# Attention heads packed two by two into 64-row tiles of the matrix array

## The chip, the cores and the metric

The kernel runs on one core of a Trainium2 chip. The metric is the device time of one execution in microseconds (us), the median of three runs. TensorE multiplies matrices, VectorE and ScalarE read its results from PSUM (eight banks of 128 partitions x 512 fp32), GpSimd works between SBUF tiles, and the sync engine issues almost all transfers.

## The reference

Two cross-attention layers follow each other on the same eight batches (B = 8, 256 query rows, C = 320, 20 heads of 16, a context of 256 rows of 512). The first 77 context rows (layer 0) or the first 252 (layer 1) are text, the rest are image rows with weights of their own.

```python
# layer 0
out_text = attend(q, k, v); out_ip = attend(q, k_ip, v_ip)      # softmax(q k^T / 4) v, 20 heads
x = (out_text + out_ip) @ Wo.T + bo + x
# layer 1
probs_t = softmax(q @ k_t.T / 4)
qsem = l2norm(probs_t @ text)                                    # 512 wide, per head and row
fused = q @ k_ip.T / 4 + 0.5 * (qsem @ l2norm(ip).T)
probs_ip = softmax(fused) * spatial_mask
x = (probs_t @ v_t + probs_ip @ v_ip) @ W_out + b_out + x
```

## The kernel before

A unit u is one batch in one layer: units 0 to 7 are layer 0 (L = 0), units 8 to 15 layer 1. Each unit is cut into ten slots j, one for a pair of heads; q = 10 u + j counts the pairs. plan(u, j) writes out by hand what every engine does in a slot, and each engine walks through the same plan and takes its own part: scores of pair q + 1, maxima of unit u + 1, `weigh` (probabilities times values, every second slot, four heads in four 32-column tiles), `weights` (exponentials), in layer 1 `quad` (the quadratic form behind the norm of qsem), 'bg' pieces of the projections of unit u + 2 (PACE says how many matmuls), `back` (transposes of the values' result), and the parts of unit u - 1 that end it ('ot', 'op' and others). 'shift' is the transposition of the maxima of unit u + 1.

Precision: a projected query or key is kept as a rounded part and the rest (hi and lo). The three products hi x hi, hi x lo and lo x hi stand one below the other as 3 x 16 = 48 rows per head. Head a of a pair has rows 48 a to 48 a + 47 of KP (keys) and of QP (queries); QP holds the two heads in two column blocks with zeros in the other head's rows, so that one matmul with 96 rows multiplies one head. Rows 96 to 99 hold the row maxima (mhi, mlo) in QP and indicators in KP: with them a matmul with 100 rows gives scores less the maximum. QP's zeros are set by GpSimd once (L1209, L1218), and rows 96 to 99 are filled with a large value at the start of layer 1 (L1241).

Lines that the change and the prediction's steps touch: L427 maxima (two matmuls of 256 columns per head), L438 transposes of the maxima, L450 scores (two matmuls of 512 columns per pair, one for each half of the keys, both heads side by side), L464 quad, L482, L486, L491 and L496 weigh, L505 back, L348 projections, L546 and L548 output. ScalarE's exponentials are L768 (rounded, PH, layer 1) and L778 (P). VectorE reduces maxima in L971 and L972 (layer 0) or L974 and L976 (layer 1) and multiplies Y by the quads in L989. GpSimd subtracts PH from P in L1198 and raises norms to the power -0.5 in L1205. On the sync queue L1294 sends the maxima into QP, L676 and L684 load packed queries and keys of unit u + 2 from DRAM, where L654 and L656 have stored them. A unit's loads come in three chunks m: pairs 0 to 3, 4 to 7, 8 and 9.

PSUM: one bank belongs to weigh, seven form a pool. take() gives the free bank that was given back longest ago and waits until its last reader is done; give() is called when the last matmul is issued. The bank of a projection is held from its first matmul to the next job's, so six take turns for the rest. A bank of scores is free when P is written, one of maxima after VectorE's second operation, one of a quad after L989, one of transposes after normalization, one of a Q projection after VectorE's lower part.

```python
MAXH = (3, 3, 3, 3, 3, 3, 2, 0, 0, 0)      # heads of maxima in each slot
MAXF = (2, 2, 2, 2, 2, 2, 2, 2, 2, 2)      # the same before unit 0
SHIFT = 7                                  # slot in which the maxima are transposed
...
bank = min((b for b in pool if id(b) not in held), key=lambda b: at.get(id(b), 0))
```

## Time and profile before

| | us |
|---|---|
| median of three runs | 886.08 (885.2 to 886.97) |
| the profiled execution | 881.61 |
| its span, first to last instruction | 879.8 |
| TensorE busy | 809.0 |
| VectorE busy | 556.6 |
| ScalarE busy | 428.3 |
| GpSimd busy | 340.7 |

The mean granted TensorE clock is 0.963 of full speed. Busy shares overlap between engines. The ends of matmuls are modelled and reach into the next ones, so the distance from one start to the next tells more than a duration.

### The profile page before, as it was taken

The numbers are of one execution on the slowest core, as the hardware profiler recorded it, in microseconds if no ns is written. First come the engines' busy times: TensorE is split into PE (matmuls) and PEld (weight loads), VectorE is DVE, ScalarE is ACT, GpSimd is POOL, SyncE is SP. The second block draws the span as 40 slices with busy tenths as digits, with TensorE's granted clock in tenths as the row PEclk, the third lists the DMA queues.
The fourth block names the chain that finished last, engine by engine and source line by source line (L and its number), as shares of the span: only waits on it lengthen the run. The fifth ranks groups of instructions, "written<-read, shape, count | busy, mean of one in ns | idle before, by whom it ended". The sixth has DMA issues, their size and how long they took to land.

```text
span 879.8 us, 17377 instructions
## 1 busy us (share of the span) xinstructions
PE 809.0 (92%) x6456; PEld 653.0 (74%) x6456; DVE 556.6 (63%) x1569; ACT 428.3 (49%) x922; POOL 340.7 (39%) x255
## 2 busy tenths in 40 slices
PE   5759799898989898999999999999999999989896
PEld 5758597676867677778787877877878778767575
DVE  4447254555555657576867848669678586596654
ACT  5234433535353536545545655455465554545451
POOL 6311101101010103031657547365384473665763
PEclk9889889999999999999999999999999999999799
DMA  9953922737262737374516234143053321401010
GB/s 267 245 125 103 213 85 64 189 116 184 70 173 81 186 97 190 95 197 113 140 39 162 85 85 122 58 110 121 26 139 97 86 83 58 111 1 34 1 30 16
DMA packets 102116, 96.71 MB, mean 110 GB/s; under 512 B 10152, under 2 KB 102032, under 8 KB 102032
## 3 DMA queue, kind: packets, MB, share of 16 engines
q1 hardware_dynamic: 100976, 94.61, 40.2%
q8 instruction: 52, 0.85, 0.4%
q10 hardware_dynamic: 1056, 0.98, 0.4%
q14 instruction: 32, 0.26, 0.1%
HBM read 57.71 MB, written 36.70 MB: 107 GB/s over the span
## 4 chain that ended last, share of the span: by engine, by line
PE 67%; DVE 9%; SPq 7%; DMA 5%; issue 5%; ACT 4%; POOL 2%; ACTq 0%; POOLq 0%; DVEq 0%
PE pB L348 19%; PE pB L464 10%; PE pB L427 7%; PE pB L450 6%; PE pB L546 5%; DMA KP<-k0d 4%; PE pPV L486 4%; PE pPV L491 3%; PE pPV L496 3%; DVE m_sb L974 3%; SPq L1294 3%; PE pPV L482 2%; PE pB L505 2%; ACT P L778 2%; POOL Y L1198 2%
## 5 line engine op out<-in xcount | busy, mean ns | idle before, releaser
L1198 POOL TENSOR_TENSOR Y<-P,wv 128x512 f32<-128x512 f32 x120 | 153.6, 1296 | 206.0 <-ACT P L778 205.9
L989 DVE TENSOR_TENSOR Y<-pB,Y 128x512 f32<-128x512 f32 x160 | 109.0, 686 | 96.0 <-PE pB L464 71.0
L427 PE MATMUL pB<-KP,QP 96*128 96x256 f32 x640 | 133.8, 292 | 25.4 <-DMA KP<-k0d 24.5
L427 PEld LDWEIGHTS pB<-KP,QP 96*128 96x128 f32 x640 | 109.1, 194 | 40.2 <-issue 18.9
L450 PE MATMUL pB<-QP,KP 100*128 100x512 f32 x320 | 114.7, 436 | 17.0 <-DMA QP<-mlo 14.2
L974 DVE TENSOR_REDUCE m_sb<-pB 128x2 f32<-128x504 f32 x160 | 108.0, 676 | 14.2 <-PE pB L427 12.4
L778 ACT ACTIVATE P<-pB 128x512 f32<-128x512 f32 x160 | 86.2, 594 | 45.9 <-PE pB L450 45.9
L1175 POOL TENSOR_TENSOR klo<-xin,khi 128x256 fp32r<-128x256 f32 x18 | 13.1, 751 | 245.5 <-ACT khi L691 245.5
L691 ACT ACTIVATE Vs<-pPV 128x512 f32<-128x512 f32 (+1 forms) x80 | 39.4, 492 | 139.0 <-PE pPV L486 106.5
L971 DVE TENSOR_REDUCE m_sb<-pB 128x2 f32<-128x154 f32 x160 | 50.0, 313 | 86.9 <-PE pB L427 86.0
L778 ACT ACTIVATE P<-pB,ln 128x512 f32<-128x512 f32 x160 | 101.3, 693 | 0.0
L768 ACT ACTIVATE wv<-pB 128x512 fp32r<-128x512 f32 x120 | 66.6, 590 | 56.0 <-PE pB L450 53.4
L972 DVE TENSOR_REDUCE m_sb<-pB 128x2 f32<-128x358 f32 x160 | 83.3, 520 | 0.0
L464 PE MATMUL pB<-wv,wk 128*128 128x512 f32 x250 | 78.3, 417 | 0.4
L348 PE MATMUL pB<-chi,wki 128*128 128x180 f32 (+3 forms) x384 | 72.0, 276 | 0.0
L450 PEld LDWEIGHTS pB<-QP,KP 100*128 100x128 f32 x320 | 52.9, 196 | 24.7 <-DMA QP<-mlo 16.1
L348 PE MATMUL pB<-khi,wq 128*128 128x256 f32 (+1 forms) x288 | 59.0, 307 | 8.5 <-DVE wq L893 8.5
L348 PE MATMUL pB<-wvi,chi 128*128 128x320 f32 x256 | 62.1, 314 | 0.4 <-POOL wvi L1188 0.4
L1205 POOL TENSOR_TENSOR rn<-n,mhalf 128x8 f32<-128x8 f32 (+2 forms) x17 | 57.4, 3379 | 11.7 <-DVE n L1020 11.7
L348 PEld LDWEIGHTS pB<-chi,wki 128*128 128x128 f32 (+1 forms) x384 | 56.8, 174 | 6.5 <-issue 4.5
L464 PEld LDWEIGHTS pB<-wv,wk 128*128 128x128 f32 x250 | 45.0, 194 | 19.5 <-issue 10.7
L348 PEld LDWEIGHTS pB<-khi,wq 128*128 128x128 f32 (+1 forms) x288 | 46.6, 195 | 14.0 <-DVE wq L893 8.5
(174 smaller groups left out, 1693.7 us busy)
## 6 DMA issues: line engine op xcount, KB each, us to landing
QP<-q0d SPq DMA_DIRECT2D x64, 192.0 KB, 4.1
KP<-k0d SPq DMA_DIRECT2D x64, 192.0 KB, 4.5
c_sb<-in_cT SPq DMA_DIRECT2D x16, 512.0 KB, 4.8
q0d<-qhi SPq DMA_DIRECT2D x32, 256.0 KB, 2.5
k0d<-khi SPq DMA_DIRECT2D x30, 256.0 KB, 2.5
q0d<-qlo SPq DMA_DIRECT2D x16, 256.0 KB, 2.8
k0d<-klo SPq DMA_DIRECT2D x15, 256.0 KB, 2.7
QP<-q1d SPq DMA_DIRECT2D x32, 96.0 KB, 4.3
```

What stands on the lines that cost most here:

```text
L348: made = mm(out, l, r, start=(n == 0), stop=(n == len(pairs) - 1))
L427: made = mm(bank[:, sc * S:sc * S + S], QP[i][0:KROWS, j, a, sc * 128:sc * 128 + 128], KP[i][0:KROWS, j, :], start=True, stop=True)
L450: mm(bank[:, :], KP[i][0:QROWS, j, ch * 128:ch * 128 + 128], QP[i][0:QROWS, j, :, :].rearrange("p a s -> p (a s)"), start=True, stop=True) ...
L464: made = mm(bank[:, :], G[i][:, col:col + 128], ph[src], start=(n == 0), stop=(n == len(jobs) - 1))
L768: act(PH[q % HR][ch], bank_of["sc", q, ch][:, :], ACT.Exp, scale=0.25).then_inc(ac_ph, 1)
L778: act(P[:, q % PR, ch, :], bank_of["sc", q, ch][:, :], ACT.Exp, scale=0.25, **twice).then_inc(ac_exp, 1)
L971: nc.vector.tensor_reduce(m_sb[:, :, h], v[:, :, 0:TXT0], AX, ALU.max)
L972: nc.vector.tensor_reduce(m_sb[:, :, H + h], v[:, :, TXT0:S], AX, ALU.max).then_inc(dv_mx, 1)
L974: nc.vector.tensor_reduce(m_sb[:, :, h], v[:, :, 0:TXT1], AX, ALU.max)
L989: tt(Y[:, p, dst, :], bank_of["gp", q, dst][:, :], Y[:, p, dst, :], MUL).then_inc(dv_y, 1)
L1198: tt(Y[:, p, ch, :], P[:, p, ch, :], PH[q % HR][ch].bitcast(F32), SUB).then_inc(po_y, 1)
L1205: tt(rn[:, :, hs], n2[:, :, hs], mhalf[:, 0:2 * n].rearrange("p (c h) -> p c h", c=2), POW).then_inc(po_rn, 1)
```

## The change

Each head of a pair gets half of the array's rows: head 0 rows 0 to 63, head 1 rows 64 to 127. KROWS becomes 48 and QROWS 52 per head, QP loses its zeros and its second column block, and every matmul of scores and maxima names a tile of 64 rows (tile_position). Each head has a PSUM bank of its own, which holds both halves of its keys (scores) or of its queries (maxima). So scores are four matmuls of 256 columns instead of two of 512, maxima four of 256 for a pair as before. Both banks of a pair are taken before its first matmul.

The order in a slot becomes scores, maxima, weigh, quads, projections, with the maxima of two heads together (MAXH and MAXF count pairs), two pairs in slots 0 and 1, one in slots 2 to 7. SHIFT goes from 7 to 8. The loads of chunks 0 and 1 stand in slot 8 of the sync program, chunk 2 stays in slot 9. Exponentials and GpSimd's difference work on one head of both key halves instead of both heads of one half, so VectorE's product waits for both differences. PH gets a tile of its own. The maxima of both heads of a pair go into QP with one DMA per row kind, two partitions each. GpSimd's three kinds of memset of QP go; an indicator of -1e20 and a row of ones take the place of the large value. Weight columns are ordered so that the four pairs of a chunk lie side by side in DRAM.

```diff
--- before.py
+++ after.py
@@ -20,8 +20,8 @@
 EC = 4
 NG = 5
 NP = H // 2
-KROWS = 96
-QROWS = 100
+KROWS = 48
+QROWS = 52
 PR = 3
 HR = 2
...
-MAXH = (3, 3, 3, 3, 3, 3, 2, 0, 0, 0)
-MAXF = (2, 2, 2, 2, 2, 2, 2, 2, 2, 2)
-SHIFT = 7
+MAXH = (2, 2, 1, 1, 1, 1, 1, 1, 0, 0)
+MAXF = (1,) * 10
+SHIFT = 8
...
-    heads = [("max", u + 1, h) for h in range(sum(many[:j]), sum(many[:j + 1]))] if u + 1 < U else []
-    first, rest = heads[:1], heads[1:]
+    pairs = [("max", u + 1, p) for p in range(sum(many[:j]), sum(many[:j + 1]))] if u + 1 < U else []
     out = []
     if 0 <= u < U - 1 and j == SHIFT:
         out += [("shift", u + 1)]
     scores = [("scores", q + 1)] if u >= 0 and q + 1 < U * NP else []
     weigh = [("weigh", *divmod(q // 2 - 1, NG))] if q >= 2 and q % 2 == 0 else []
     weigh += [("weights", q + 1)] if scores else []
+    out += scores + pairs + weigh
     if u >= B:
-        out += scores + weigh + [("quad", q, 0)] + first + [("quad", q, 1)]
-    else:
-        out += scores + first + weigh
-    out += pieces[0] + pieces[1] + rest[:1] + pieces[2] + rest[1:]
+        out += [("quad", q, 0), ("quad", q, 1)]
+    out += pieces[0] + pieces[1] + pieces[2]
     if q >= 2 and q % 2 == 0:
         out += [("back", *divmod(q // 2 - 1, NG))]
...
-        QP = [sb(f"QP{i}", [128, NP, 2, S], F32R) for i in range(2)]
+        QP = [sb(f"QP{i}", [128, NP, S], F32R) for i in range(2)]
         KP = [sb(f"KP{i}", [128, NP, S], F32R) for i in range(2)]
...
-        PH = [[flat(wv)[:, 896 + 512 * i:896 + 512 * i + 512] for i in range(2)], [flat(w)[:, at:at + 512] for w, at in ((wv, 1920), (wk, 1792))]]
+        PH = sb("PH", [128, HR, 2, 2 * S], F32R)
...
         def ind_ready(u):
             u = u if u < 2 else B + u % 2 if u >= B else u % 2
-            return l_ind[u], 16
+            return l_ind[u], 64 if u >= B else 32
...
-            def maximum(u, h):
-                i, j, a = u % 2, h // 2, h % 2
-                bank = take("mx", u * H + h)
-                pe.wait_ge(*pack_landed(u, h // 8))
-                pe.wait_ge(po_set, 2 + u % 2)
+            def maxima(u, j):
+                i = u % 2
+                banks = [take("mx", u * H + 2 * j + a) for a in range(2)]
+                pe.wait_ge(*pack_landed(u, j // 4))
                 for sc in range(2):
-                    made = mm(bank[:, sc * S:sc * S + S], QP[i][0:KROWS, j, a, sc * 128:sc * 128 + 128],
-                              KP[i][0:KROWS, j, :], start=True, stop=True)
-                made.then_inc(pe_mx, 1)
-                give(bank)
+                    for a in range(2):
+                        rows = slice(64 * a, 64 * a + KROWS)
+                        made = mm(banks[a][:, sc * S:sc * S + S], QP[i][rows, j, sc * 128:sc * 128 + 128],
+                                  KP[i][rows, j, :], start=True, stop=True, tile_position=(64 * a, 0))
+                        if sc == 1:
+                            made.then_inc(pe_mx, 1)
+                            give(banks[a])
...
+                banks = [take("sc", q, a) for a in range(2)]
                 for ch in range(2):
-                    bank = take("sc", q, ch)
-                    mm(bank[:, :], KP[i][0:QROWS, j, ch * 128:ch * 128 + 128],
-                       QP[i][0:QROWS, j, :, :].rearrange("p a s -> p (a s)"), start=True, stop=True).then_inc(pe_sc, 1)
-                    give(bank)
+                    for a in range(2):
+                        rows = slice(64 * a, 64 * a + QROWS)
+                        made = mm(banks[a][:, ch * S:ch * S + S], KP[i][rows, j, ch * 128:ch * 128 + 128],
+                                  QP[i][rows, j, :], start=True, stop=True, tile_position=(64 * a, 0))
+                        if ch == 1:
+                            made.then_inc(pe_sc, 1)
+                            give(banks[a])
...
-                ph = PH[q % HR]
...
-                    made = mm(bank[:, :], G[i][:, col:col + 128], ph[src], start=(n == 0), stop=(n == len(jobs) - 1))
+                    made = mm(bank[:, :], G[i][:, col:col + 128], PH[:, q % HR, src, :], start=(n == 0), stop=(n == len(jobs) - 1))
...
         def head_rows(dram, m):
             chunk = dram[m // 2][m % 2]
-            return chunk.rearrange("z (d j a) s -> (z d) j a s", a=2, d=D)
...
         def load_queries(engine, dma, u, m):
             i, js = u % 2, slice(4 * m, min(4 * m + 4, NP))
             engine.wait_ge(l_q, 96 * (u + 1))
-            engine.wait_ge(po_set, 2 + i)
             if u >= 2:
                 engine.wait_ge(pe_sc, 2 * ((u - 2) * NP + js.stop))
             for a in range(2):
-                dma(QP[i][48 * a:48 * a + 48, js, a, :].bitcast(F32), head_rows(qd[u], m)[:, :, a, :]).then_inc(l_ld[i][m], 16)
+                dma(QP[i][64 * a:64 * a + KROWS, js, :].bitcast(F32), head_rows(qd[u], m)[:, a]).then_inc(l_ld[i][m], 16)
...
-                dma(KP[i][48 * a:48 * a + 48, js, :].bitcast(F32), head_rows(kd[u], m)[:, :, a, :]).then_inc(l_ld[i][m], 16)
...
             def rounded_weights(q):
                 k = q - B * NP
-                for ch in range(2):
-                    ac.wait_ge(pe_sc, 2 * q + ch + 1)
+                for a in range(2):
+                    ac.wait_ge(pe_sc, 2 * q + a + 1)
                     ac.wait_ge(pe_gp, 2 * (k - HR) + 2)
                     ac.wait_ge(po_y, 2 * (k - HR) + 2)
-                    ac.wait_ge(pe_bg, job_no(B - 1, "V2"))
-                    act(PH[q % HR][ch], bank_of["sc", q, ch][:, :], ACT.Exp, scale=0.25).then_inc(ac_ph, 1)
+                    act(PH[:, q % HR, :, S * a:S * a + S], two(bank_of["sc", q, a], 128, 2), ACT.Exp, scale=0.25).then_inc(ac_ph, 1)
...
                 twice = {"bias": ln2[:, 0:1]} if q >= B * NP else {}
-                for ch in range(2):
-                    ac.wait_ge(pe_sc, 2 * q + ch + 1)
+                for a in range(2):
+                    ac.wait_ge(pe_sc, 2 * q + a + 1)
                     ac.wait_ge(pe_pv, (q - PR) // 2 + 1)
                     ac.wait_ge(lo_w["ki0"], 1)
                     ac.wait_ge(lo_w["v0"], 1)
                     ac.wait_ge(dv_set, 1)
-                    act(P[:, q % PR, ch, :], bank_of["sc", q, ch][:, :], ACT.Exp, scale=0.25, **twice).then_inc(ac_exp, 1)
+                    act(P[:, q % PR, :, S * a:S * a + S], two(bank_of["sc", q, a], 128, 2), ACT.Exp, scale=0.25,
+                        **twice).then_inc(ac_exp, 1)
...
             def maximum(u, h):
-                n = u * H + h
+                n, col = u * H + h, h % 2 * NP + h // 2
                 v = bank_of["mx", n][:, :].rearrange("p (c t) -> p c t", c=2)
                 dv.wait_ge(pe_mx, n + 1)
                 dv.wait_ge(pe_sr, u)
                 if u < B:
-                    nc.vector.tensor_reduce(m_sb[:, :, h], v[:, :, 0:TXT0], AX, ALU.max)
-                    nc.vector.tensor_reduce(m_sb[:, :, H + h], v[:, :, TXT0:S], AX, ALU.max).then_inc(dv_mx, 1)
+                    nc.vector.tensor_reduce(m_sb[:, :, col], v[:, :, 0:TXT0], AX, ALU.max)
...
             def quad(q, dst):
                 k, p = q - B * NP, q % PR
                 dv.wait_ge(pe_gp, 2 * k + dst + 1)
-                dv.wait_ge(po_y, 2 * k + dst + 1)
+                dv.wait_ge(po_y, 2 * k + 2)
                 tt(Y[:, p, dst, :], bank_of["gp", q, dst][:, :], Y[:, p, dst, :], MUL).then_inc(dv_y, 1)
...
                         if what == "max":
-                            maximum(*a)
+                            for h in range(2):
+                                maximum(a[0], 2 * a[1] + h)
...
             def weights(q):
                 k, p = q - B * NP, q % PR
-                for ch in range(2):
-                    po.wait_ge(ac_exp, 2 * q + ch + 1)
-                    po.wait_ge(ac_ph, 2 * k + ch + 1)
+                for a in range(2):
+                    ss = slice(S * a, S * a + S)
+                    po.wait_ge(ac_exp, 2 * q + a + 1)
+                    po.wait_ge(ac_ph, 2 * k + a + 1)
                     po.wait_ge(pe_pv, (q - PR) // 2 + 1)
                     po.wait_ge(lo_w["k1"], 1)
                     po.wait_ge(lo_w["v1"], 2)
-                    tt(Y[:, p, ch, :], P[:, p, ch, :], PH[q % HR][ch].bitcast(F32), SUB).then_inc(po_y, 1)
+                    tt(Y[:, p, :, ss], P[:, p, :, ss], PH[:, q % HR, :, ss].bitcast(F32), SUB).then_inc(po_y, 1)
...
-            nc.gpsimd.memset(QP[0][:, :, :, :].bitcast(F32), 0.0).then_inc(po_set, 1)
-            po.wait_ge(po_set, 2)
...
-            po.wait_ge(lo_w["vi0"], 1)
-            nc.gpsimd.memset(QP[1][:, :, :, :].bitcast(F32), 0.0).then_inc(po_set, 1)
-            po.wait_ge(po_set, 3)
...
-                    if u in (B - 1, B) and j == 3:
-                        po.wait_ge(pe_sc, 2 * u * NP)
-                        po.wait_ge(*((lo_c, 4 * (B + 2)) if u < B else (po_y, 10)))
-                        nc.gpsimd.memset(QP[(u + 1) % 2][KROWS:QROWS, :, :, :].bitcast(F32), 1e20).then_inc(po_big, 1)
-                        po.wait_ge(po_big, u - B + 2)
...
-                sp.wait_ge(po_set, 2 + i)
...
-                dma(KP[i][KROWS:QROWS, :, :].bitcast(F32),
-                    ind[:, L, None, :].to_broadcast([4, NP, S]).bitcast(F32)).then_inc(l_ind[u], 16)
+                for a in range(2):
+                    dma(KP[i][64 * a + KROWS:64 * a + QROWS, :, :].bitcast(F32),
+                        ind[:, L, None, :].to_broadcast([4, NP, S]).bitcast(F32)).then_inc(l_ind[u], 16)
+                    if L:
+                        sp.wait_ge(dv_set, 1)
+                        dma(QP[i][64 * a + KROWS + 2:64 * a + KROWS + 3, :, :].bitcast(F32),
+                            ones[0:2 * NP, :]).then_inc(l_ind[u], 16)
...
-                sp.wait_ge(po_set, 2 + i)
-                if u in (B, B + 1):
-                    sp.wait_ge(po_big, u - B + 1)
-                rows = [(96, mhi, 0), (98, mhi, H), (97, mlo, 0), (99, mlo, H)] if u < B else [(96, mhi, 0), (97, mlo, 0)]
+                rows = [(0, mhi, 0), (2, mhi, H), (1, mlo, 0), (3, mlo, H)] if u < B else [(0, mhi, 0), (1, mlo, 0)]
                 for r, tile, h0 in rows:
                     sp.wait_ge(ac_sr, u + 1)
                     if tile is mlo:
                         sp.wait_ge(dv_sr, u + 1)
-                    dma(QP[i][r:r + 1, :, :, :].bitcast(F32), tile[h0:h0 + H, :].bitcast(F32)).then_inc(l_m[i], 16)
+                    dma(QP[i][KROWS + r:128:64, :, :].bitcast(F32), tile[h0:h0 + H, :].bitcast(F32)).then_inc(l_m[i], 16)
...
-                    if u + 2 < U and j == NP - 1:
-                        for m in range(KC):
+                    for m in ((0, 1) if j == 8 else (2,) if j == NP - 1 else ()):
+                        if u + 2 < U:
                             load_queries(sp, dma, u + 2, m)
                             load_keys(sp, dma, u + 2, m)
-                        if u + 2 in (1, B, B + 1):
-                            load_ind(u + 2)
+                    if u + 2 in (1, B, B + 1) and j == NP - 1:
+                        load_ind(u + 2)
...
-    ind[2, 1, TXT1:S] = -1.0
+    ind[2, 1, TXT1:S] = -1e20
...
-    order = _np.concatenate([_np.arange(128 * m, min(128 * m + 128, C)).reshape(-1, D).T.reshape(-1) for m in range(3)])
+    order = _np.concatenate([_np.arange(128 * m, min(128 * m + 128, C)).reshape(-1, 2, D).transpose(2, 1, 0).reshape(-1)
+                             for m in range(3)])
     P = lambda a: _np.ascontiguousarray(a[:, order])
```

## Rows read from the trace of the kernel before

**Rows 1.** The page, part 1: busy time, share of the span, instructions.

```profile
PE 809.0 (92%) x6456; PEld 653.0 (74%) x6456; DVE 556.6 (63%) x1569; ACT 428.3 (49%) x922; POOL 340.7 (39%) x255
```

**Rows 2.** Windows: length, busy PE, PEld, DVE, ACT, POOL, clock, DMA share, GB/s.

```profile
247.00:291.00 44.00, 39.55 (x343) 32.56 (x343) 24.89 (x74) 20.17 (x45) 4.83 (x8) 0.96 0.47 127
...
643.00:701.00 58.00, 57.83 (x453) 46.09 (x451) 41.58 (x118) 31.05 (x67) 31.85 (x22) 1.00 0.33 93
```

**Rows 3.** The waits: who for whom, us in total, times, longest.

```profile
PE pB L427 <- DMA KP<-k0d: 24.5, 8, 5.3
...
PE pB L450 <- DMA QP<-mlo: 14.2, 8, 5.4
```

**Rows 4.** The chain in order of time: start, us, engine and line, matmuls.

```profile
430.82 0.24 PE pB L427 x2
...
432.22 0.47 PE pB L450 x2
...
508.47 0.43 PE pB L548 x2
...
510.37 0.86 PE pPV L496 x16
```

**Rows 5.** Timeline of PE at start-up: start, us, line, form, count.

```profile
16.79 0.38 PE L348 MATMUL pB<-chi,wki 128*128 128x180 f32 x2
...
17.13 0.38 PE L348 MATMUL pB<-chi,wki 128*128 128x180 f32 x2
```

**Rows 6.** Timeline of PE in slot 6 of unit 9, from full array to column tiles and back.

```profile
508.98 0.39 PE L450 MATMUL pB<-QP,KP 100*128 100x512 f32 x1
509.30 1.07 PE L491 MATMUL pPV<-P,VY 128*32 128x256 f32 x16
510.18 1.05 PE L496 MATMUL pPV<-Y,y 128*32 128x256 f32 x16
511.16 1.21 PE L464 MATMUL pB<-wv,wk 128*128 128x512 f32 x4
```

**Rows 7.** Timeline, all engines, end of unit 4 and start of unit 5.

```profile
279.66 0.38 PE L438 MATMUL pB<-ident,m_sb 128*40 128x128 f32 x2 [0.90 <-DVE m_sb L972]
...
281.95 0.62 PE L450 MATMUL pB<-QP,KP 100*128 100x512 f32 x2
...
283.42 1.47 SPq L1294 DMA_DIRECT2D QP<-mlo  x2
...
286.29 2.08 SPq L684 DMA_DIRECT2D KP<-k0d  x2
...
286.64 0.73 PE L450 MATMUL pB<-QP,KP 100*128 100x512 f32 x2 [0.54 <-DMA QP<-mlo]
...
288.08 0.62 PE L450 MATMUL pB<-QP,KP 100*128 100x512 f32 x2
...
291.72 0.47 PE L427 MATMUL pB<-KP,QP 96*128 96x256 f32 x2 [3.02 <-DMA KP<-k0d]
```

**Rows 8.** The page, part 6: DMA issues, KB each, median us to landing.

```profile
KP<-k0d SPq DMA_DIRECT2D x64, 192.0 KB, 4.5
...
k0d<-khi SPq DMA_DIRECT2D x30, 256.0 KB, 2.5
```

**Rows 9.** Timeline of DVE, two heads of maxima in layer 0.

```profile
263.86 0.32 DVE L971 TENSOR_REDUCE m_sb<-pB 128x2 f32<-128x154 f32 x1
...
264.53 0.31 DVE L971 TENSOR_REDUCE m_sb<-pB 128x2 f32<-128x154 f32 x1
```

**Rows 10.** Timeline, all engines, slots 9 and 0 around unit 12.

```profile
644.61 5.54 POOL L1205 TENSOR_TENSOR rn<-n,mhalf 128x32 f32<-128x32 f32 x1 [0.58 <-DVE n L1020]
...
650.13 3.79 POOL L1198 TENSOR_TENSOR Y<-P,wv 128x512 f32<-128x512 f32 x3
...
651.52 0.69 DVE L989 TENSOR_TENSOR Y<-pB,Y 128x512 f32<-128x512 f32 x1 [2.41 <-POOL Y L1198]
...
652.52 0.91 PE L450 MATMUL pB<-QP,KP 100*128 100x512 f32 x2
```

9 lines of the change are left out of this document (6 added, 3 removed).

## The prediction

> **What bounds the kernel now.** I read the busy shares of the page first, then the windows by unit, then the chain of waits, then single slots of the timeline. TensorE is busy 92% of the span, no other engine above 63% [rows 1]. By windows the two halves differ: a layer-0 unit of 44.0 us has TensorE busy 39.55 us, a layer-1 unit 57.83 of 58.00 us, with VectorE at 41.58 and GpSimd at 31.85 [rows 2]. So in layer 1 every matmul taken away is time, until another wait appears; in layer 0 there are about 4.5 us of waits per unit that two DMA chains and a reduction set: eight waits each for packed keys (24.5 us) and for shift rows (14.2 us) [rows 3]. TensorE is thus the engine to shorten, and the question is what comes late once it is shorter.
>
> **Matmuls removed.** The chain shows two score matmuls (512 columns) in 0.47 us and the two of one head's maxima (256 columns) in 0.24 us: 0.235 and 0.12 us each [rows 4]. After the change both kinds are four matmuls of 256 columns per pair of heads, in two row tiles. If the two tiles run at once, each four cost 2 x 0.12 = 0.24 us. Scores: 160 pairs x (0.47 - 0.24) = 37 us. Maxima: 160 pairs x (0.48 - 0.24) = 38 us. Together -75 us.
> Row tiles are nowhere in this trace, so the cost is bounded. Low end: column tiles, 16 fp32 matmuls of 256 columns in 0.86 us [rows 4], that is 0.054 us each; one such matmul alone takes 0.215 us (L548: two in 0.43 us), so four stream at once. Upper end: weight loads that don't overlap. Matmuls of 180 columns with a full load of 128 columns each come every 0.11 us (three from 16.79 to 17.13 [rows 5]), though by their columns (0.12 us for 256) they would need 0.085: the load paces them. Four such loads in a row would be 0.45 us. I take 0.24 us, since the column rows are of the same kind and show loads and matmuls of different tiles starting together.
> The Trainium skill ("TensorE: Matmul & The Clock Gate", Part 3, The mechanism) states that a weight load overlaps matmuls in flight only where its row group differs, and that matmuls of different row tiles start about 4 ns apart. By it the four would take 0.24 us and the sum stays at -75; by loads in a row as in [rows 5] it would be -8. No row here shows a row tile.
>
> **Mode changes added.** From the last score matmul (508.98) to the first column-tiled one (509.30) are 0.32 us instead of 0.235; the way back, L496 at 510.18 to L464 at 511.16, is 0.98 us for four quads of 0.22: about 0.09 us each way [rows 6]. Now a unit changes to column tiles and back five times, 10 changes. Afterwards each of the ten slots enters row tiles, five go on to column tiles and then to full, five go straight to full: 25. Fifteen more x 16 units + 20 in unit -1 = 260 x 0.09 = +23 us. TensorE's work: -52 us, about 3.35 us per unit.
>
> **Layer 0: shift and loads.** Rows around 280 us, between units 4 and 5 [rows 7]. The transposes of the maxima (L438) start at T = 279.66, the shift DMAs come behind the key stores of the slot before (the mlo pair at 283.42), and scores(u+1, 0) starts at 286.64 = T + 7.0 after a wait of 0.54. The loads stand directly behind the shift rows in sync's order, so already now they are issued right after them: the loop moves them to slot 8, but SHIFT moves to slot 8 too, so nothing is sooner; all is one slot later on TensorE's count. After the change T is the start of slot 8: the key stores are out of the way, mhi is ready about T + 0.8 (an estimate: transpose 0.38 and a copy of 40x256, 0.4), four DMAs of 0.75 us each (1.47 for two) are issued by T + 4.0, the last from T + 3.25, and it lands 2.45 us later as now (half into the x2 row, 284.2, to 286.64): T + 5.7, perhaps 0.4 more, since each of them now writes two partitions instead of one, which no row shows. TensorE's slot 8 lasts 4.1 us (281.95 to 286.64 less 0.54), so it waits 1.6 to 2.0 instead of 0.54: +1.2. Keys: Q, Q, K, K at 0.65 us each (1.25 for two are 0.62 and a pause) from T + 4.0; the second K is issued at T + 6.0 and lands 4 us later (4.5 is the median [rows 8]; in the row here 287.8 to 291.7), T + 10.0. TensorE is there at T + 5.7 + 1.44 (slot 9, 286.64 to 288.08) + 0.24, T + 7.4: a gap of 2.6 for 3.02. Rows of four heads are now contiguous in DRAM, so packets may grow; stores of 256 KB land in 2.5 us against 4.5 for these 192 KB [rows 8], so between 0 and 2 us could come off; I take none, since the loads queue behind each other either way. L438's own wait, 0.90, should fall to 0.3, as the last pair is now ahead of eleven background matmuls.
> Slots 0 and 1 now hold four heads each (MAXH 2, 2). VectorE takes 0.67 us a head (263.86 to 264.53 [rows 9]). By the rule of take(), the oldest free bank of seven with one held by the background chain, the fourth maximum of slot 1 gets the bank of the transposes that closed slot 0 (free after their normalization, for which I take 0.9 us, between one head's maxima and two [rows 9]; wait 0.4), and the pair of slot 2 gets a bank of Qa, whose low part VectorE writes behind the four maxima: 0.9 + 4 x 0.67 + 0.68 = 4.3 us into a slot that TensorE leaves after about 3.4: 0.9 us. Sum per unit: +1.2 - 0.4 - 0.6 + 0.4 + 0.9 = +1.5, for the seven steady units, with some 2 us for the first ones: +12 us.
>
> **Layer 1: the same two slots.** In slot 0 of unit 12, which ends at 652.52, GpSimd's power takes 5.54 us, so that the differences Y of one pair (1.26 us each) are ready only at 651.4 and 652.7, and VectorE's product waits 2.41 us for the first [rows 10]. After the change the halves are heads, each product needs both, and the first comes 1.3 us later. TensorE in slot 0: weigh starts after the maxima, ScalarE's P comes behind weigh's evacuation, and the second quad needs the bank of the first score: about 0.5 us. In slot 1 the first pair waits for the banks of both products, the second for the transposes that are normalized behind them: with the slot's start at 652.9, the products done at 653.4 and 654.1 and the bank free at 654.85 (0.75 later, the same estimate without its sum), TensorE loses 0.25 us before the first pair and 1.1 before the second. The old order loses about 0.45 us in that slot as well, where its first quad needs the bank of the last product. The keys of the next unit: issued by T + 4.5, landing T + 8.5, wanted at T + 8.1: 0.4. Per unit 0.5 + 1.35 - 0.45 + 0.4 = +1.8, six units: +11 us. VectorE does not become the bound over a whole unit: 41.6 us of work in some 56 [rows 2]. Units 14 and 15, which wait for GpSimd now: the later product costs 0.7 us in some five places, +3 us.
> The memsets of QP on GpSimd go; in the start-up ScalarE and the loads set the time and nothing waits for them, so 0. ScalarE's and GpSimd's operations on two pieces of 256 instead of one of 512 keep their elements; I take 0 (ScalarE's share, 49% [rows 1], would cover some per cent).
>
> **Sum.** -75 + 23 + 12 + 11 + 3 = -26 us. The profiled execution has 879.8 us of span and 881.61 in all; the median of the runs is 886.08. -26 of 881.6 is 855.6; the runs lie 4.5 higher: 860, and since the waits were counted in the busiest places only, 862.
>
> **Rivals.** (a) The tiles don't overlap, or their weight loads don't. For: a 128-column load alone is 0.11 us and each half tile loads 128 columns. Against: the column tiles. Then scores and maxima gain 0.02 to 0.03 us a pair, 8 us at most, and changes and waits stay: -8 + 23 + 26 = +41, 927 us.
> (b) The slower side with the mechanism intact: the rotation of banks. Scores and two pairs take six of seven banks at once in slots 0 and 1, so TensorE runs at the pace of VectorE's reductions (0.67 us a head) and of ScalarE's exponentials. I have 1.5 to 1.8 us per unit; from 3.35 us per unit the change gives nothing. If the lag reaches slot 2 and weigh waits for the products too, 4 us per unit x 15 = 60 against 52: +8, 894 us. For: two fronts of four maxima, 2.7 us of VectorE ahead of the products. Against: VectorE idles there now (2.41 us ahead of the product [rows 10]).
> The Trainium skill ("TensorEngine Tiling (Array Packing)", Gotcha 1) states that row tiling raises the pressure on PSUM because row tiles write different banks; that speaks for this rival, and no row of the kernel before shows how much.
> (c) The waits are mostly covered: larger packets end the key gap 1 us sooner and VectorE fills its idle time with maxima. Waits of +8 instead of +26: -44, 842 us.
> (d) That the loads come a slot sooner, as the change says: then layer 0 would lose its key gap, 3 us x 7, and end at 862 - 18 = 844, which is (c)'s time by another way; sync's order speaks against it, so its chance is counted in (c)'s.
>
> **How the numbers follow.** The forecast -26 has a chance of 0.58, with its own range of 848 to 876; (c) 0.15, (b) 0.12, (a) 0.15. Runs of this kernel differ by about 0.2%, 1.8 us, which is what can be told from no change. Of the forecast's case 0.03 ends within that; so faster 0.70, same 0.03, slower 0.27. The range reaches from (c) to (b) and leaves (a) out: 840 to 896.
>
> **What would show it.** L427 and L450 (as they are renumbered) in the chain: four matmuls in 0.24 us means tiles at once; 0.45 means loads in a row. The gap before the first key-dependent maximum in layer 0 near 2.6 us, the gap before scores(u+1, 0) near 1.8. In layer 1 TensorE's share falls from 0.997 to about 0.97 in a unit of 57, with the loss in slot 1. If that slot is no longer than before, (c) holds; if VectorE's products end the waits of weigh, (b).

## The result and the profile after

The changed kernel takes 892.4 us (median of 8 runs, 887.9 to 893.7) beside 886.4 us (8 runs of the kernel before in the same session, 882.9 to 889.2): a ratio of 1.0066, 95% interval 1.0045 to 1.0087. It is slower; the forecast was 862 us, 3% faster. The profiled executions stand a little further apart than the medians: 892.19 us with a span of 890.4 against 881.61 with 879.8, +10.6 us. The accounts below are of these two. Of one kernel below, grouped, two of the four executions were over 1.5% above its fastest: its median (1015.3 us) is of all four, its ratio of the other two.

Lines are renumbered by the change: scores are L452, maxima L426, transposes of the maxima L438, quads L467, projections L346.

The page of the changed kernel, busy time and share, answers to [rows 1]:

```profile
PE 791.7 (89%) x6776; PEld 607.8 (68%) x6776; DVE 554.5 (62%) x1569; ACT 433.1 (49%) x922; POOL 321.8 (36%) x251
```

TensorE is busy 17 us less, where 52 were forecast, and its share falls by three points, so waits have come in. The windows of one whole unit each (from the first score matmul of a unit to that of the next; length, busy PE, PEld, DVE, ACT, POOL, granted clock, DMA share, GB/s) answer to [rows 2]. First the kernel before, unit 5 and unit 13:

```profile
286.64:330.60 43.96, 39.54 (x343) 32.71 (x343) 26.04 (x77) 20.88 (x47) 4.19 (x6) 0.96 0.51 141
701.87:760.63 58.76, 58.59 (x460) 46.85 (x459) 42.28 (x120) 31.34 (x68) 32.60 (x23) 1.00 0.29 79
```

and the same units of the changed kernel:

```profile
283.33:326.82 43.49, 39.06 (x365) 30.36 (x365) 25.90 (x78) 21.19 (x47) 4.14 (x7) 0.92 0.56 143
709.68:768.95 59.27, 57.15 (x478) 44.18 (x477) 42.35 (x119) 31.52 (x67) 32.44 (x23) 1.00 0.32 80
```

In layer 1 TensorE works 1.44 us less per unit, not 3.35, and idles 1.95 us more. In layer 0 it gains 0.5 us, and its mean clock falls from 0.96 to 0.92. TensorE's waits (engine, tile and line, releaser: total us, times, longest) answer to [rows 3]:

```profile
PE pB L426 <- DMA KP<-k0d: 25.0, 10, 5.7
PE pB L452 <- DMA QP<-mlo: 21.8, 9, 8.5
...
PE pB L426 <- DVE qlo L895: 4.0, 7, 0.6
PE pB L426 <- DVE Y L991: 3.5, 6, 2.0
...
PE pB L467 <- DVE alo L895: 3.0, 5, 1.2
PE pB L426 <- DVE ST L1016: 3.0, 5, 0.7
PE pB L426 <- DVE klo L895: 2.8, 5, 0.6
PE pB L438 <- DVE m_sb L974: 2.7, 7, 0.6
...
PE pB L467 <- ACT P L779: 2.5, 6, 0.7
PE pB L426 <- DVE tb L1009: 2.3, 8, 0.3
```

The wait for shift rows grew by 7.6 us against [rows 3], and seven kinds of wait behind VectorE and ScalarE that hardly existed before make 21.1 us (4.0 + 3.5 + 3.0 + 3.0 + 2.8 + 2.5 + 2.3); the wait ahead of the transposes (L438) fell from 6.1 to 2.7. All idle times of TensorE over 0.25 us together are 94.1 us, before 66.0: +28.

**What a mode change costs.** Slot 9 of unit 7 has no maxima and the same six background matmuls in both kernels. Timeline of PE (start, us, line, form, count), before:

```profile
411.05 0.71 PE L450 MATMUL pB<-QP,KP 100*128 100x512 f32 x2
411.60 0.28 PE L348 MATMUL pB<-chi 128*128 128x256 f32 x1
...
412.32 0.63 PE L450 MATMUL pB<-QP,KP 100*128 100x512 f32 x2
```

and after:

```profile
412.59 0.50 PE L452 MATMUL pB<-QP,KP 52*128 52x256 f32 x4 [0.17 <-DMA QP<-mlo]
413.03 0.39 PE L346 MATMUL pB<-chi 128*128 128x256 f32 x1
413.25 0.28 PE L346 MATMUL pB<-clo,chi 128*128 128x256 f32 x1
413.37 0.28 PE L346 MATMUL pB<-chi,clo 128*128 128x256 f32 x1
...
413.73 0.28 PE L346 MATMUL pB<-chi,clo 128*128 128x256 f32 x1
413.94 0.50 PE L452 MATMUL pB<-QP,KP 52*128 52x256 f32 x4
```

Background matmuls of 256 columns follow each other every 0.12 us (413.25 to 413.37). The first one after the row tiles is followed by the second only after 0.22 us (413.03 to 413.25), and the first tile matmul starts 0.21 us after the last full one (413.73 to 413.94). A change thus costs twice: about 0.1 us ahead of the first matmul in the new mode, and 0.1 us again ahead of the second. The slot is 1.35 us for 1.27: the scores take 0.235 us less and two changes come, 0.16 us each here, because the kernel before has a pause of its own in this slot, behind the transposes (411.05 to 411.60 is 0.55 us for two matmuls of 0.235). In the other slots read this way it is up to 0.20 us. The medians of all such steps at full clock in the changed kernel's trace agree: 0.21 us for 0.12 up to the first matmul in the new mode, 0.22 for 0.12 up to the second (from column tiles back to quads 0.34 for 0.23). Counted in the traces, PE changes its mode 160 times before and 419 times after: 259 more.

**The half clock.** Windows of one microsecond of the changed kernel in slot 0 of unit 4, after TensorE idled from 242.9 to 245.2 for packed keys (columns as above; the granted clock is the third last):

```profile
245.00:246.00 1.00, 0.80 (x12) 0.70 (x16) 0.29 (x2) 0.00 (x0) 1.00 (x2) 0.91 1.09 217
246.00:247.00 1.00, 1.00 (x12) 0.45 (x13) 1.00 (x4) 0.00 (x0) 0.11 (x1) 0.50 1.03 209
...
249.00:250.00 1.00, 1.00 (x9) 1.00 (x9) 0.00 (x0) 1.00 (x3) 0.00 (x0) 0.89 1.08 284
250.00:251.00 1.00, 1.00 (x10) 0.88 (x8) 0.00 (x0) 0.29 (x1) 0.00 (x0) 1.00 0.23 69
```

Some 3.4 us run at 0.50, the lower of the clock's two levels (1.2 GHz instead of 2.4), once the wait is over; the price is about half of that. Other stretches of the changed kernel behind waits for keys last 6.8 us. The kernel before has 3.4 us behind four of its six waits for keys in units 2 to 7, and none behind those of units 6 and 7 (2.80 and 2.56 us). Over the span the granted clock is 0.963 before and 0.950 after: (1 - 0.963) x 879.8 = 32.6 us of full-speed time lost against (1 - 0.950) x 890.4 = 44.5, +12 us. What of it falls into idle time costs nothing, so 12 is an upper bound. Laid over TensorE's busy time alone, the clock of the two traces loses 28.7 us before and 34.9 after: +6. The busy time without that loss is 780.3 and 756.8 us, 23.5 less; below this is called the work at full speed. Idle time of every length is 70.9 and 98.7 us, so -23.5 + 27.8 + 6.2 = +10.5 is the whole difference.

### The profile page after: what moved, and what is told of

Read it like the earlier page. It is cut to its first block, busy times and chain, and to the rows that moved or that the text cites. A ratio compares the mean times of both kernels' runs of the same rounds, so it can differ in the third digit from the quotient of the medians.

```text
span 890.4 us, 18142 instructions
## 1 busy us (share of the span) xinstructions
PE 791.7 (89%) x6776; PEld 607.8 (68%) x6776; DVE 554.5 (62%) x1569; ACT 433.1 (49%) x922; POOL 321.8 (36%) x251
## 4 chain that ended last, share of the span: by engine, by line
PE 66%; DVE 13%; DMA 8%; SPq 4%; issue 4%; ACT 3%; POOL 1%; ACTq 0%; POOLq 0%; DVEq 0%
PE pB L346 20%; PE pB L467 13%; DMA KP<-k0d 6%; PE pB L549 5%; PE pB L426 5%; PE pB L452 4%; PE pPV L494 4%; PE pPV L489 4%; PE pPV L499 4%; PE pPV L485 2%; PE pB L508 2%; SPq L1289 2%; DVE m_sb L974 2%; DVE Y L991 1%; DVE m_sb L973 1%
## 5 line engine op out<-in xcount | busy, mean ns | idle before, releaser
L1202 POOL TENSOR_TENSOR Y<-P,PH 128x512 f32<-128x512 f32 x160 | 202.6, 1290 | 230.2 <-ACT P L779 230.1
L991 DVE TENSOR_TENSOR Y<-pB,Y 128x512 f32<-128x512 f32 x160 | 105.5, 686 | 65.3 <-PE pB L467 47.4
L769 ACT ACTIVATE PH<-pB 128x512 fp32r<-128x512 f32 x160 | 86.5, 594 | 62.8 <-PE pB L452 56.1
L426 PE MATMUL pB<-KP,QP 48*128 48x256 f32 x640 | 72.3, 310 | 41.9 <-DMA KP<-k0d 25.0
L452 PE MATMUL pB<-QP,KP 52*128 52x256 f32 x640 | 81.7, 335 | 24.7 <-DMA QP<-mlo 21.8
L467 PE MATMUL pB<-PH,wk 128*128 128x512 f32 x350 | 97.0, 413 | 4.0 <-DVE alo L895 2.6
L426 PEld LDWEIGHTS pB<-KP,QP 48*128 48x128 f32 x640 | 52.6, 198 | 51.8 <-issue 39.4
L452 PEld LDWEIGHTS pB<-QP,KP 52*128 52x128 f32 x640 | 48.8, 189 | 56.4 <-issue 25.2
L467 PEld LDWEIGHTS pB<-PH,wk 128*128 128x128 f32 x350 | 61.5, 189 | 32.5 <-issue 15.3
L346 PE MATMUL pB<-chi,wki 128*128 128x180 f32 (+3 forms) x384 | 70.2, 277 | 0.0
L346 PE MATMUL pB<-khi,wq 128*128 128x256 f32 (+1 forms) x288 | 58.1, 315 | 8.9 <-DVE wq L895 8.9
L346 PE MATMUL pB<-wvi,chi 128*128 128x320 f32 x256 | 62.7, 319 | 0.4 <-POOL wvi L1191 0.4
L346 PEld LDWEIGHTS pB<-chi,wki 128*128 128x128 f32 (+1 forms) x384 | 55.5, 172 | 8.8 <-issue 4.5
L1209 POOL TENSOR_TENSOR rn<-n,mhalf 128x8 f32<-128x8 f32 (+2 forms) x17 | 57.4, 3379 | 9.7 <-DVE n L1022 9.7
L467 PE MATMUL pB<-PH,wv 128*128 128x512 f32 x210 | 58.4, 416 | 1.5 <-ACT P L779 1.0
```

Source lines behind the costliest of these rows:

```text
L346: made = mm(out, l, r, start=(n == 0), stop=(n == len(pairs) - 1))
L426: made = mm(banks[a][:, sc * S:sc * S + S], QP[i][rows, j, sc * 128:sc * 128 + 128], KP[i][rows, j, :], start=True, stop=True, tile_positi ...
L452: made = mm(banks[a][:, ch * S:ch * S + S], KP[i][rows, j, ch * 128:ch * 128 + 128], QP[i][rows, j, :], start=True, stop=True, tile_positi ...
L467: made = mm(bank[:, :], G[i][:, col:col + 128], PH[:, q % HR, src, :], start=(n == 0), stop=(n == len(jobs) - 1))
L769: act(PH[:, q % HR, :, S * a:S * a + S], two(bank_of["sc", q, a], 128, 2), ACT.Exp, scale=0.25).then_inc(ac_ph, 1)
L991: tt(Y[:, p, dst, :], bank_of["gp", q, dst][:, :], Y[:, p, dst, :], MUL).then_inc(dv_y, 1)
```

## The experiments

Every run is beside runs of the kernel before on the same chip; intervals are of that ratio. The kernel before had medians of 886.4 us beside the changed kernel, 887.9 beside full_new_order, more_changes, grouped and slot1_maxima, 885.2 beside loads_slot9, by_layer, by_layer_even and by_layer_shift7, and 889.1 beside extra_beside, extra_apart, by_layer_long and before_slot1, so medians of different groups can be off against each other by some 3 us.

| kernel | median us | ratio to before (95%) |
|---|---|---|
| changed kernel | 892.4 | 1.0066 (1.0045 to 1.0087) |
| full_new_order | 902.9 | 1.0182 (1.0150 to 1.0213) |
| more_changes | 919.0 | 1.0337 (1.0277 to 1.0397) |
| extra_beside | 911.4 | 1.0283 (1.0233 to 1.0332) |
| extra_apart | 948.0 | 1.0686 (1.0642 to 1.0729) |
| grouped | 1015.3 | 1.1354 (1.1299 to 1.1408) |
| loads_slot9 | 889.3 | 1.0045 (1.0016 to 1.0074) |
| slot1_maxima | 906.6 | 1.0223 (1.0191 to 1.0255) |
| by_layer | 878.0 | 0.9916 (0.9888 to 0.9944) |
| by_layer_even | 898.6 | 1.0148 (1.0111 to 1.0186) |
| by_layer_shift7 | 881.7 | 0.9966 (0.9932 to 0.9999) |
| by_layer_long | 875.9 | 0.9876 (0.9829 to 0.9922) |
| before_slot1 | 857.1 | 0.9652 (0.9605 to 0.9698) |

**The two halves of the change apart (full_new_order).** The kernel before with its full-array matmuls, in the new order:

```diff
-MAXH = (3, 3, 3, 3, 3, 3, 2, 0, 0, 0)
+MAXH = (4, 4, 2, 2, 2, 2, 2, 2, 0, 0)
...
-SHIFT = 7
+SHIFT = 8
...
+    out += scores + heads + weigh
...
-    out += pieces[0] + pieces[1] + rest[:1] + pieces[2] + rest[1:]
+    out += pieces[0] + pieces[1] + pieces[2]
...
-                    if u + 2 < U and j == NP - 1:
-                        for m in range(KC):
+                    for m in ((0, 1) if j == 8 else (2,) if j == NP - 1 else ()):
```

> The kernel before, full-array matmuls and its layout of QP and KP, with only the order of the change: the heads of the maxima two by two behind the scores (4, 4, 2, 2, 2, 2, 2, 2, 0, 0 heads by slot), the shift in slot 8, the loads split over slots 8 and 9. Its distance to the kernel before is the price of the order, its distance to the changed kernel what tiles bring net. If a mode change costs 0.2 us, tiles bring -75 + 260 x 0.2 = -23 and this kernel takes about 892 + 23 = 915 us, some us less where its slower matmuls cover waits. If it costs 0.09 us, tiles bring -52 and this kernel takes about 944 us.

Measured: 902.9 us. The order alone costs 1.8%, 16 us, and the tiles give back 902.9 - 892.4 = 10.5, together with what came with them (the layout of QP and KP, exponentials and differences by head, fewer DMAs), which no run takes apart. That is far from the 52 of the forecast. The two traces say where it went, from this run to the changed kernel: work at full speed -26.3 us, where 75 us of matmuls less and 259 changes of 0.2 more make -23; idle time +10.6, as a faster TensorE meets more waits (those over 0.25 us are 82.3 us here and 94.1 with tiles); half clock in busy time +5.3. The sum is -10.4, as the spans have it (900.8 and 890.4). Slot 7 of unit 12 shows the same: scores at 711.18 and 715.16, 3.98 us, against 3.91 in the changed kernel (700.47 to 704.38, below). Tiles take 0.475 us out of it and the two changes put (3.91 - 3.98 + 0.475) = 0.41 back.

**More changes, no work (more_changes).**

```diff
-    out += scores + pairs + weigh
+    out += scores + pieces[0] + pairs + weigh
...
-    out += pieces[0] + pieces[1] + pieces[2]
+    out += pieces[1] + pieces[2]
```

> The changed kernel with the first third of each slot's background matmuls placed between the scores and the maxima, so that the array goes from row tiles to the full array and back once more in eight slots of the units 0 to 13: 14 x 8 x 2 = 224 mode changes more, no work added. The theory that a change costs 0.2 us (0.1 at the first matmul in the new mode and 0.1 at the second) expects 224 x 0.2 = +45, less some 4 us because the background matmuls cover 0.5 us of each wait for packed keys: about 933 us. The rival, that a change costs 0.09 us as in the prediction and the loss lies in waits for VectorE and for DMAs, expects +20 - 4: about 908 us.

Measured: 919.0 us, +26.6, between the two, so the median alone decides nothing. (The edit adds 238 changes and not 224: slot 8, without maxima, gets one more as well; the trace counts 657 for 419.) The single slots decide. Slot 7 of unit 12 in the changed kernel:

```profile
700.47 0.51 PE L452 MATMUL pB<-QP,KP 52*128 52x256 f32 x4
700.81 0.40 PE L426 MATMUL pB<-KP,QP 48*128 48x256 f32 x4
...
704.38 0.39 PE L452 MATMUL pB<-QP,KP 52*128 52x256 f32 x2
```

and in more_changes, with the same matmuls:

```profile
730.89 0.50 PE L452 MATMUL pB<-QP,KP 52*128 52x256 f32 x4
...
731.88 0.50 PE L426 MATMUL pB<-KP,QP 48*128 48x256 f32 x4
...
735.18 0.39 PE L452 MATMUL pB<-QP,KP 52*128 52x256 f32 x2
```

4.29 us for 3.91: two changes, 0.19 each. Slots 5 and 6 grow alike (6.88 to 7.26, 7.72 to 8.10), slot 8 with its one change from 5.30 to 5.48. In slots 3 and 4 of layer 1, where TensorE waits for VectorE, the time falls (5.04 to 4.75, 8.15 to 7.70), and in layer 0 in slot 0, where it waits for keys. So nearly 0.2 us a change holds in slots without waits, and part of it is hidden where a wait stands behind it. By the traces the span grew by 33.6 us (this profiled execution was the slowest of four): work at full speed +37.2, or 0.156 us a change, idle time -12.7, half clock in busy time +9.1.

**The same matmuls, beside and apart (extra_beside, extra_apart).** 126 unused row-tile matmuls in each; the two differ only in their place:

```diff
-    out += scores + pairs + weigh
+    out += scores + pairs + ([("extra", q + 1)] if 0 <= u < U - 2 and j != 8 else []) + weigh        (extra_beside)
...
-    out += pieces[0] + pieces[1] + pieces[2]
+    out += pieces[0] + ([("extra", q + 1)] if 0 <= u < U - 2 and j != 8 else []) + pieces[1] + pieces[2]     (extra_apart)
```

> The changed kernel with one more matmul of 256 columns in a row tile right behind the scores and maxima of nine slots of the units 0 to 13 (126 in all, into the oldest free bank, its result unused): no mode change more. 126 x 0.12 = +15 us, and some us for a bank that is asked for early: about 910 us. It is the base for the run beside it.

> As extra_beside, the same 126 matmuls, but each behind the first third of its slot's background matmuls, so that the array changes to row tiles and back twice more per slot: 252 changes. Against extra_beside: +50 us if a change costs 0.2 us, +23 us if it costs 0.09 us, less by what falls into slots that wait for VectorE anyway (in more_changes nearly half of it did).

Measured: 911.4 and 948.0 us, 36.5 us for 252 changes (419 and 671 by the traces). Slot 7 of unit 12 in extra_beside, where L461 is scores and L438 the unused matmul:

```profile
716.49 0.51 PE L461 MATMUL pB<-QP,KP 52*128 52x256 f32 x4
716.83 0.41 PE L426 MATMUL pB<-KP,QP 48*128 48x256 f32 x4
717.08 0.28 PE L438 MATMUL pB<-QP,KP 48*128 48x256 f32 x1
...
720.53 0.39 PE L461 MATMUL pB<-QP,KP 52*128 52x256 f32 x2
```

and in extra_apart:

```profile
758.28 0.50 PE L461 MATMUL pB<-QP,KP 52*128 52x256 f32 x4
...
760.91 0.28 PE L346 MATMUL pB<-chi,clo 128*128 128x256 f32 x1
761.12 0.38 PE L438 MATMUL pB<-QP,KP 48*128 48x256 f32 x1
761.43 0.39 PE L346 MATMUL pB<-chi 128*128 128x256 f32 x1
761.65 0.28 PE L346 MATMUL pB<-clo,chi 128*128 128x256 f32 x1
...
762.68 0.39 PE L461 MATMUL pB<-QP,KP 52*128 52x256 f32 x2
```

First, four maxima matmuls in tiles take 717.08 - 716.83 = 0.25 us in the steady state: two tiles at once, as predicted. Second, the slot takes 4.04 us beside and 4.40 apart, and the rows show where: 760.91 to 761.65 is 0.74 us for three steps that take 0.12 each without a change, so two changes cost 0.38. Over the whole kernel it is 36.5 / 252 = 0.145. That number is a mixture: between the traces idle time falls by 12.2 us, half clock in busy time grows by 14.4, and the work at full speed grows by 36.9, 0.146 us a change. Why this is less than the 0.19 of single slots is not shown; in slots of layer 1 with waits the step is smaller than 0.38 (slot 4 of unit 12: 8.44 to 8.61 us).

**Fewer changes (grouped).** Scores and maxima of odd slots at the slot's end, quads behind the background matmuls:

```diff
+    late = j % 2 == 1 and u >= 0
+    quads = [("quad", q, 0), ("quad", q, 1)] if u >= B else []
+    if not late:
+        out += scores + pairs + weigh
+    out += pieces[0] + pieces[1] + pieces[2] + quads
...
+    if late:
+        out += scores + pairs + weigh
```

> The changed kernel with scores and maxima of every odd slot moved to that slot's end, so that they touch the scores and maxima of the even slot behind it, and the quads moved behind the background matmuls: 5 x 2 changes fewer per unit, 160 in all, no work removed. If a change costs 0.2 us: -32 us; in slot 9 the background matmuls also cover the wait for the shift rows, about 1 us in each of 7 units, and eight banks wanted at once in slot 0 cost some 1 us per unit: together about 865 us. If a change costs 0.09 us: -14, about 880 us. If banks become the bound, it is slower than 892 us.

Measured: 1015.3 us. Banks became the bound, the third of the answers. TensorE between slots 1 and 2 of unit 12 (scores are L455):

```profile
755.94 0.80 PE L455 MATMUL pB<-QP,KP 52*128 52x256 f32 x4 [3.66 <-ACT P L782]
```

It stands 3.66 us before the second scores until ScalarE has emptied a bank, and from 755 to 759 its windows give the clock as 0.50. TensorE's waits over 0.25 us make 169 us, and its mean clock is 0.877, both in the profiled execution, which took 1020.2 us. The trace counts 291 changes, 128 fewer and not 160, and the work at full speed is 21 us less, 0.165 us a change: the mode changes did give their time back, and idle time (+75 us) and the half clock in busy time (+74) took far more. Two scores and two pairs of maxima side by side ask for eight banks (2 x 2 + 2 x 2), and seven rotate.

**The loads (loads_slot9).**

```diff
-for m in ((0, 1) if j == 8 else (2,) if j == NP - 1 else ()):
+for m in (range(KC) if j == NP - 1 else ()):
```

> The changed kernel with all loads of Q and K back in slot 9. The theory that the loads' move brings nothing, because sync issues them behind the shift rows either way, expects the same time in the steady units, and the start 3 us sooner because the loads of unit 1 no longer stand ahead of the shift rows of unit 0: about 889 us, 892 at most. The rival, that the loads really start a slot sooner in the change, expects each wait for packed keys longer by about a slot's 3 to 5 us: over 915 us.

Measured: 889.3 us, ratio 1.0045 (1.0016 to 1.0074), which overlaps with the changed kernel's 1.0066 (1.0045 to 1.0087): the move gains nothing. It shifts a wait at the start. Sync's DMAs of the changed kernel:

```profile
54.82 0.89 SPq L686 DMA_DIRECT2D KP<-k0d  x2
...
57.17 1.03 SPq L1289 DMA_DIRECT2D QP<-mlo  x2
```

Loads of unit 1 go out ahead of the shift rows of unit 0, and TensorE's first scores wait 8.46 us, 4.96 with the loads in slot 9 and 5.36 in the kernel before. But with the loads in slot 9 TensorE then waits 2.71 us for the keys of unit 1 (2.86 in the kernel before), which the changed kernel doesn't. The score matmuls that open unit 2 start at 154.93 in the changed kernel and at 155.16 here: the start is not 3 us sooner in the end, as was expected.

**Where the maxima stand (slot1_maxima, by_layer, by_layer_even, by_layer_long, by_layer_shift7).** Pairs by slot, for the units up to 8 / from 9 on (`MAXH[u > B]` picks one where there are two):

```diff
-MAXH = (2, 2, 1, 1, 1, 1, 1, 1, 0, 0)                                        in all units, SHIFT = 8
+MAXH = (0, 2, 2, 2, 1, 1, 1, 1, 0, 0)                                        slot1_maxima
+MAXH = ((0, 2, 2, 2, 1, 1, 1, 1, 0, 0), (2, 2, 1, 1, 1, 1, 1, 1, 0, 0))      by_layer
+MAXH = ((0, 2, 2, 2, 1, 1, 1, 1, 0, 0), (1, 1, 2, 1, 2, 1, 1, 1, 0, 0))      by_layer_even
+MAXH = ((0, 1, 2, 1, 2, 1, 2, 1, 0, 0), (2, 2, 1, 1, 1, 1, 1, 1, 0, 0))      by_layer_long
+MAXH = ((0, 2, 2, 2, 2, 1, 1, 0, 0, 0), (2, 2, 1, 1, 1, 1, 1, 1, 0, 0))      by_layer_shift7, SHIFT = 7 up to unit 8
```

> The changed kernel with the maxima of the next unit begun in slot 1 instead of slot 0 (pairs 0, 2, 2, 2, 1, 1, 1, 1, 0, 0 by slot). The number of mode changes stays, since slot 0 keeps its scores. The theory that the wait for packed keys in slot 0 is wholly a loss expects its 1.9 to 3.9 us in units 1 to 8 gone, about -21 us: 871 us. The rival, that VectorE's reductions then pile up in slots 1 to 3 and give it back in waits for PSUM banks, expects no less than 885 us.

Measured: 906.6 us, on the side of the rival (885 or more). It hides a split. Windows of a layer-0 and a layer-1 unit of slot1_maxima:

```profile
237.18:277.11 39.93, 36.68 (x365) 28.85 (x365) 25.03 (x76) 20.80 (x47) 4.57 (x7) 1.00 0.55 140
718.80:783.39 64.59, 58.73 (x478) 45.71 (x477) 42.64 (x119) 31.45 (x67) 32.41 (x23) 0.97 0.28 73
```

The layer-0 unit takes 39.9 us where the changed kernel needs 42.4 (240.91 to 283.33): the wait for keys has gone, and the half clock behind it with it (clock 1.00). The layer-1 unit is 5.3 us longer: TensorE idles 5.9 us in it for 2.1, in waits for VectorE's results and for P, and 3% of the clock is lost. That four maxima per slot on VectorE in slots 1 to 3, beside the products, are the reason is the likely reading, not a separate result. So each half got its own pattern.

> The changed kernel with the pairs of maxima 0, 2, 2, 2, 1, 1, 1, 1, 0, 0 by slot in the units up to 8 (the ones that wait for packed keys in slot 0) and 2, 2, 1, 1, 1, 1, 1, 1, 0, 0 as in the change in the units 9 to 14. In slot1_maxima the units 2 to 7 took 12.6 us less than in the changed kernel and unit 8 2.5 us less, the units 9 to 13 5.4 us more each. If the two halves are independent: 892 - 15 = 877 us, faster than the kernel before. If VectorE hands the later maxima on to the next units, 885 us or more.

Measured: 878.0 us, as expected, and 0.8% faster than the kernel before.

> As by_layer, with 1, 1, 2, 1, 2, 1, 1, 1, 0, 0 pairs by slot in the units 9 to 14, so that in slots 0 and 1 VectorE has two maxima instead of four ahead of or behind the products. If the waits of slot 1 (0.65 us for the bank of the transposes, 0.3 us for P) come from four maxima in a row on VectorE, as predicted, they go and a layer-1 unit loses about 1 us: 872 us. If they come from the later product alone (both halves of Y needed), nothing is gained: 877 us or some more, since slots 2 and 4 then have two pairs beside the low parts of the projections.

Measured: 898.6 us, 20 us worse than by_layer: neither answer. Slots 0 and 1 became 0.9 and 0.5 us shorter, but slot 2 went from 6.6 to 11.4 us. Rows of the timeline there, unit 12:

```profile
668.15 0.34 ACT L800 ACTIVATE ex<-t 128x160 f32<-128x160 f32 x1 [3.51 <-DVE t L1038]
...
668.39 1.07 ACT L769 ACTIVATE PH<-pB 128x512 fp32r<-128x512 f32 x2
...
670.37 2.80 PE L467 MATMUL pB<-PH,wk 128*128 128x512 f32 x7 [2.11 <-ACT P L779]
```

TensorE reaches the slot sooner than VectorE: ScalarE waits 3.51 us for VectorE's softmax of the image tokens, its exponentials for the quads stand behind that, TensorE waits 2.11 us for them and then runs at half clock (0.50 from 672 to 674). In layer 1 the double pairs belong into slots 0 and 1, where the change put them.

> As by_layer, with 0, 1, 2, 1, 2, 1, 2, 1, 0, 0 pairs in the units up to 8, so that the double pairs stand in slots 2, 4 and 6, the long ones. If the waits for banks of slots 2 and 3 (0.45, 0.42 and 0.85 us behind low and high parts on VectorE) come from eight to twelve maxima in a row, 1 us per unit goes: 870 us. If not, 878 us or some more.

> As by_layer, with 0, 2, 2, 2, 2, 1, 1, 0, 0, 0 pairs in the units up to 8 and their shift in slot 7, the loads of the first eight pairs right behind it. The wait for the shift rows (0.5 to 1.5 us per unit in layer 0) goes and the keys come a slot sooner: about 877 - 8 = 869 us. If VectorE does not get through four slots of four maxima, they come back as waits for banks: 880 us or more.

Measured: 875.9 us for by_layer_long, whose interval overlaps with by_layer's, and 881.7 us for by_layer_shift7. An earlier shift does not end the wait for shift rows (1.12 us ahead of unit 4, 0.81 in by_layer): the transposes are made at 231.12, but sync issues the key stores from 231.16 to 234.65 and the shift rows only then, as [rows 7] shows of the kernel before. A layer-0 unit is 40.0 us in the first, 40.5 in the second, 39.9 in by_layer.

**The same step without tiles (before_slot1).** The kernel before with one edit, the maxima one slot later up to unit 8 and spread anew, SHIFT still 7:

```diff
-MAXH = (3, 3, 3, 3, 3, 3, 2, 0, 0, 0)
+MAXH = ((0, 3, 4, 3, 4, 3, 3, 0, 0, 0), (3, 3, 3, 3, 3, 3, 2, 0, 0, 0))
...
-    many = MAXF if u < 0 else MAXH
+    many = MAXF if u < 0 else MAXH[u > B]
```

> The kernel before, full-array matmuls, with one change: in the units up to 8 the maxima start in slot 1 (0, 3, 4, 3, 4, 3, 3, 0, 0, 0 heads by slot instead of 3, 3, 3, 3, 3, 3, 2). It loses six waits for packed keys of 2.4 to 3.0 us and the stretches at half clock behind them (1.2 to 1.6 us each): -26, 860 us. If this comes true, most of what by_layer gained is the place of the maxima and not the tiles. If the full-array kernel gains little because VectorE's maxima pile up, 880 us or more, and the tiles are needed for it.

Measured: 857.1 us, ratio 0.9652 (0.9605 to 0.9698): faster than both kernels, and than every kernel with tiles. Its page and the windows of units 5 and 13:

```profile
PE 798.8 (93%) x6456; PEld 647.3 (76%) x6456; DVE 556.3 (65%) x1569; ACT 426.6 (50%) x922; POOL 341.2 (40%) x255
...
268.51:307.44 38.93, 37.62 (x346) 31.66 (x344) 25.87 (x76) 20.73 (x47) 4.26 (x6) 1.00 0.57 160
676.21:734.96 58.75, 58.57 (x460) 46.90 (x459) 42.33 (x120) 31.29 (x68) 32.59 (x23) 1.00 0.29 78
```

In units 2 to 5 some five us each have gone, in unit 5 3.1 of idle time (4.42 to 1.31, the keys above all) and 1.9 of busy time (39.54 to 37.62), nearly all of it the same work at full clock. Unit 7 gains 2.0 us and unit 6 nothing. TensorE's waits over 0.25 us are 51.2 us for 66.0, and the time lost to the half clock is (1 - 0.974) x 855.0 = 22 us for 32.6. Together that is 25 us, and the span is 24.8 us shorter. The medians of this group are further apart, 889.1 and 857.1: the profiled execution of the kernel before was one of its fastest. With tiles the best order tried stays 19 us behind: a unit of layer 0 takes 40.0 us in by_layer_long for 38.9 here, unit 8 57.4 for 53.9, a unit of layer 1 59.3 for 58.8. The pauses of the mode changes and the maxima that stand in pairs beside scores are in all of them; how the 19 us divide between the two was not tried.

## Why the prediction was wrong

**What bounds the kernel: right.** TensorE's time is the time in layer 1, and layer 0 had the waits.

**Matmuls removed, -75: right.** Four tile matmuls take 0.25 us beside each other, and by the trace of the changed kernel nine in ten of its pairs start 1 to 6 ns apart. Rival (a), at 927 us, falls.

**Mode changes added, +23: the step that failed.** From [rows 6] the distance to the first matmul in the new mode was read, 0.09 us over the usual step, and taken for the whole cost. The second matmul in the new mode comes 0.1 us late as well. The kernel before shows it too, in the line behind the quads of [rows 6]:

```profile
512.21 0.41 PE L427 MATMUL pB<-KP,QP 96*128 96x256 f32 x2
```

From 511.16 to 512.21 four quads take 1.05 us, where four steps of 0.235 are 0.94. The pair extra_beside and extra_apart confirms it (0.38 for two changes). 260 changes are 260 x 0.2 = 52 us, not 23: 29 us of the error. The measured work at full speed fell by 23.5 us, and -75 + 52 is -23. The Trainium skill ("TensorEngine Tiling (Array Packing)", Key Properties) states that a change of tiling mode drains TensorE; the traces agree in so far as TensorE pauses at each change, and give 0.16 to 0.20 us for it.

**Layer 0 waits, +12: the total near, its parts wrong.** Up to the end of unit 7 idle time grew by 9 us. Predicted were +1.5 us per unit; over units 2 to 5 together it grew by 0.2. Between units 4 and 5 the changed kernel waits 0.35, 1.05, 2.23, 0.29 and 0.55 us (transposes, shift rows, keys, slot 1, slot 2), 4.47 in all, the kernel before 4.46 [rows 7], as the shift rows arrive sooner than worked out (T + 5.4 instead of T + 5.7, with a longer slot 8 in front of them), and the two bank waits are 0.3 us shorter than taken. The first two waits for shift rows are longer, 8.46 and 7.44 us for 5.36 and 5.20: +5.3 where 2 were taken; 3 of them are the loads ahead of the shift rows, which loads_slot9 showed, and 2.5 come back because the 2.86 us for the keys of unit 1 become 0.36 a unit later. Missed altogether: in layer 1 the old order had weigh and a quad ahead of the first maxima, and unit 8 waited for no keys. Now maxima come first:

```profile
418.37 1.22 PE L426 MATMUL pB<-KP,QP 48*128 48x256 f32 x8 [3.94 <-DMA KP<-k0d]
```

That is +3.9, and unit 7 adds 0.8. It is the order and not the tiles: full_new_order waits 2.51 us at the same place.

**Layer 1 waits, +1.8 per unit: the size right, in part by luck.** Unit 13 has four waits over 0.25 us, 1.94 in all:

```profile
721.17 0.50 PE L426 MATMUL pB<-KP,QP 48*128 48x256 f32 x4 [0.65 <-DVE ST L1016]
...
738.05 0.50 PE L426 MATMUL pB<-KP,QP 48*128 48x256 f32 x4 [0.56 <-DVE klo L895]
```

The other two are 0.27 for P in slot 1 and 0.46 for a low part in slot 3. The size is as forecast and half of the places are: slot 1 loses 0.92 us, slots 3 and 4, not named, the rest. The 0.5 us of slot 0 and the 0.4 for keys did not come in this unit, nor did the kernel before have the 0.45 us that were taken off: it has no wait over 0.25 us in unit 13. Units 14 and 15 wait 3.7 us more than before, for 3 predicted. All waits together are +28 where 26 were predicted.

**Left out: the clock.** The sum had no term for TensorE's clock. More stretches at half clock cost 6 us of busy time (28.7 to 34.9), by the clock of the traces.

**The sum.** -75 + 52 + 28 + 6 = +11, and the span grew by 10.6. Of the 37 us between that and the forecast of -26, the mode changes are 29, the clock 6 and the waits 2.

**The rivals.** The time is near rival (b)'s 894, but not by its mechanism: it needed 4 us of waits per unit in the unchanged sum, and 1.9 were there. Rival (c) and (d) fall; loads a slot sooner bring nothing, as sync's order had said. The bank rotation of (b) is real, though: grouped, the one way round the mode changes that was tried, needed eight banks.

## What to carry to other kernels

Read the price of a mode change of TensorE over two matmuls, not one, and count the changes before the matmuls: here four matmuls saved 0.235 us per slot and kind, and going there and back cost 0.4, so short runs of tile matmuls between full-array ones hardly pay. A wait of TensorE has to be priced with the half clock that may follow: behind the waits for keys of 2.4 to 3.0 us in the kernel before it added 1.7 us each in four units of six. Moving the maxima so that the first needs its load one slot later, with nothing else changed, gave 3.5%. When a change has two halves, run each alone: the order cost 16 us and the tiles brought 10.

## What the hardware showed unasked

Half-clock stretches were longer in the kernels with unused matmuls added. Behind the wait for keys in unit 4 of extra_apart TensorE was busy nearly all the time and still ran at 0.50 through the 9 us shown (10.2 by the clock's record), where the changed kernel came back after 3.4:

```profile
266.00:275.00 9.00, 8.68 (x52) 5.91 (x52) 2.75 (x8) 1.57 (x3) 1.62 (x3) 0.50 0.64 133
```

Behind the waits for keys of units 2 to 8 the stretches are 3.4 or 6.8 us in the changed kernel, 6.8 in extra_beside, and 6.8 or 10.2 in extra_apart. So more changes cost more than their own pauses in a kernel that also waits, but extra_beside has no more changes than the changed kernel and is longer too; why the clock stays low there, no run here tells. Loads of four heads with contiguous rows did not get faster in the changed kernel: 5.6 us to landing for K against 4.5 [rows 8]; full_new_order, with the old layout and the new order, has 4.7, and what makes the difference was not tried.
